# Retiming the small pieces between the layers of a fused two-layer network on one Trainium2 core

## The reference

```
# layer 0: wavelet filters and linear attention, and a gated network
xn   = layernorm(x)
low, highs = two levels of dwconv(4 taps)[:, ::2] on xn
q    = elu(h) + 1;  k = q;  v = h                 # h: low, 16 heads of 16
num  = q (k^T v);   den = q . sum(k) + 1e-6;  low = num / den
low  = synthesis by dwconv of repeated low and highs; y = layernorm(xn + low)
h    = silu(xn W1 s1) * (xn W2 s2)                # 1024 wide
g    = gelu(h H1 s);  g = gelu(g H2 s)            # 1024 x 1024, twice
x2   = x + y * silu(g W3 s)
# layer 1: selective state space with 16 states, feed-forward, 8 experts of which 2
xn   = layernorm(..); delta = softplus(xn Wd + bd); B, C = xn Wbc
h_t  = exp(delta A) h_(t-1) + delta xn B_t;  y_t = h_t . C_t;  s = y + D xn
s   += gelu(layernorm(s) W1 + b1) W2 + b2          # 256 -> 1024 -> 256
nf   = rmsnorm(x');  top 2 of 8 logits, softmax of the two -> combine weights
moe  = sum over chosen experts of mlp2(clipped swiglu(mlp1(nf)))
out  = x2 + s * silu(x' + moe)
```

## Time and profile before

| | before |
|---|---|
| median of 3 runs | 1803.55 us |
| profiled execution | 1803.55 us, its span 1801.8 us |
| PE matmul busy | 1456.6 us (81%) |
| DVE busy | 1386.9 us (77%) |
| ACT busy | 1142.9 us (63%) |
| POOL busy | 973.2 us (54%) |
| mean granted TensorE clock | 0.92 of full speed |

### The profile page before, as it was taken

The page is one execution under the profiler, slowest core; times in us unless marked ns, Lnnn a source line. Parts: engine busy times, 40 slices in busy tenths (PEclk is TensorE's granted clock), DMA queues, the critical chain, the costliest instruction groups (busy, mean ns, idle before and its releaser), DMA issues. The chain is left out here.

```text
span 1801.8 us, 16539 instructions
## 1 busy us (share of the span) xinstructions
PE 1456.6 (81%) x5296; PEld 628.9 (35%) x5296; DVE 1386.9 (77%) x1736; ACT 1142.9 (63%) x1575; POOL 973.2 (54%) x616
## 2 busy tenths in 40 slices
PE   4899889899888789899897779889897764654676
PEld 1354334344333234434343324434343221111232
DVE  2683268899688878889688878989678869989844
ACT  3536678777527668868527668878526754465565
POOL 2132164667009775757008875756107864784854
PEclk9999999999999889999999989999999885686989
DMA  8001000000201000000201000000100200000000
GB/s 197 1 10 50 1 12 1 24 1 1 82 0 36 24 24 1 24 1 0 82 0 36 24 24 1 19 6 1 70 12 15 114 24 0 1 1 0 0 12 12
DMA packets 12600, 42.43 MB, mean 24 GB/s; under 512 B 1866, under 2 KB 1890, under 8 KB 10466
## 3 DMA queue, kind: packets, MB, share of 16 engines
q1 hardware_dynamic: 11698, 35.08, 5.3%
q0 software_dynamic: 816, 6.30, 1.6%
HBM read 38.23 MB, written 4.19 MB: 24 GB/s over the span
## 5 line engine op out<-in xcount | busy, mean ns | idle before, releaser
L795 POOL TENSOR_TENSOR gate<-gate,lin 128x512 f32<-128x512 f32 x120 | 154.8, 1290 | 346.2 <-DVE lin L2407 341.2
L772 POOL TENSOR_TENSOR gx<-gx,sy 128x1024 f32<-128x1024 f32 x120 | 292.7, 2439 | 37.9 <-DVE sy L2288 33.0
L1171 ACT ACTIVATE gate<-gate 128x512 f32<-128x512 f32 x128 | 80.2, 627 | 163.2 <-DVE gate L2396 163.0
L1531 PE MATMUL psf<-g1p,h2w 128*128 128x512 f16 x768 | 182.2, 386 | 0.6 <-ACT tf L958 0.6
L750 POOL TENSOR_TENSOR g2p<-tf,g2p 128x512 fp32r<-128x512 f32 x64 | 86.1, 1351 | 163.7 <-ACT g2p L981 163.7
L2255 DVE TENSOR_TENSOR psu<-so,psu 128x1024 f32<-128x1024 f32 x128 | 156.5, 1223 | 17.8 <-PE psu L1655 17.0
L1078 ACT ACTIVATE da<-delta,aneg 128x512 f32<-128x512 f32 x256 | 163.5, 710 | 4.3 <-DVE st L2272 3.7
L2272 DVE TENSOR_TENSOR_SCAN st<-da,carry,psu 128x512 f32<-128x512 f32 x128 | 156.8, 1267 | 8.4 <-ACT carry L1093 6.6
L1817 PE MATMUL psu<-ap,mw 128*128 128x512 f16 x384 | 109.0, 413 | 54.3 <-POOL ap L800 54.2
L2272 DVE TENSOR_TENSOR_SCAN st<-da,psu 128x512 f32<-128x512 f32 x128 | 149.1, 1206 | 1.9 <-issue 0.3
L800 POOL TENSOR_TENSOR ap<-gate,ap 128x512 f16<-128x512 f32 x116 | 142.9, 1234 | 0.0
(11 more groups left out here) (395 smaller groups left out, 3359.3 us busy)
## 6 DMA issues: line engine op xcount, KB each, us to landing
mw<-in_mlp_w SPq DMA_DIRECT2D x3, 2048.0 KB, 8.0
xn<-in_x SPq DMA_DIRECT2D x8, 512.0 KB, 5.9
wf<-in_wf SPq DMA_DIRECT2D x4, 1024.0 KB, 4.8
xr<-in_x SPq DMA_DIRECT2D x8, 512.0 KB, 3.7
x<-gx SPq DMA_DIRECT2D x8, 512.0 KB, 3.8
out<-outc SPq DMA_DIRECT2D x8, 512.0 KB, 3.1
mw<-in_mlp_w SPq DMA_DIRECT2D x3, 1024.0 KB, 10.1
h1w<-in_h POOLq DMA_DIRECT2D x1, 2048.0 KB, 12.7
```

The source lines that it names most:

```text
L772: pool.tensor_tensor(out, chunk(gx, c), sy[:, n % 2], ALU.add).then_inc(y_acc.sem, 1)
L795: pool.tensor_tensor(gate[:, r % NG], gate[:, r % NG], lin_at(b, r)[:], ALU.mult)\
L1531: last = pe.matmul(banks[m], w[:, t, cols], src[:, half, t], start=(t == 0 and half == 0), stop=(t == KF - 1 and half == 1))
```

## The change

Only numbers change: at which step of a stage some small pieces stand. No instruction's operands change, no DMA moves on SP, and SP's order is the same. The number of ACT's table loads, which follows from the order, goes from 251 to 262.

```diff
@@ constants of the schedule @@
 NEXT_AT, NEXT_CENTER_AT, NEXT_SQ_AT, NEXT_VAR_AT, NEXT_STD_AT, NEXT_SCALE_AT, NEXT_SPLIT_AT, NEXT_LOW_AT = \
-    26, 27, 28, 31, 31, 33, 32, 32
+    26, 27, 28, 29, 30, 32, 33, 33
-LI_AT, LI_SQ_AT, LI_VAR_AT, LI_ROOT_AT, LI_SCALE_AT, LI_SPLIT_AT, LI_LOW_AT = 5, 6, 7, 9, 9, 10, 11
+LI_AT, LI_SQ_AT, LI_VAR_AT, LI_ROOT_AT, LI_SCALE_AT, LI_SPLIT_AT, LI_LOW_AT = 6, 7, 8, 9, 9, 10, 11
 LF_SQ_AT, LF_VAR_AT, RMS_AT, Q_AT, RMS1_AT, ATTN_AT, LOGITS_AT, NUM_AT, EXP_AT, TURN_AT, TURN1_AT = \
-    0, 2, 3, 5, 5, 7, 7, 9, 9, 13, 13
+    0, 2, 3, 4, 5, 6, 7, 8, 9, 10, 12
@@ POOL, batch, expert stage @@
-((10, l0_product, 0), (11, l0_out, 0), (13, l0_product, 1), (16, l0_out, 1))
+((8, l0_product, 0), (10, l0_out, 0), (15, l0_product, 1), (16, l0_out, 1))
@@ ACT, opening, chunk 1 @@
-((7, l0_std, 1), (7, head_root, 0), (9, split_input, 1), (10, head_affine, 0), (13, softplus, 0), (13, head_b16, 0))
+((7, l0_std, 1), (8, head_root, 0), (9, split_input, 1), (10, head_affine, 0), (12, softplus, 0), (13, head_b16, 0))
@@ ACT, batch, expert stage @@
-(24, softplus)
+(23, softplus)
@@ ACT, closing, chunk 0 @@
-((2, head_square, 1), (1, expert_root, 0), ...
+((1, head_square, 1), (1, expert_root, 0), ...
@@ PE, batch, expert stage @@
-(8, lb_average, 1) ... (14, head_mean)
+(7, lb_average, 1) ... (13, head_mean)
@@ PE, closing, chunk 1 @@
-(7, expert_turn, 1)
+(6, expert_turn, 1)
@@ DVE, opening @@
-(2, lb_center, 0)
+(1, lb_center, 0)
@@ DVE, batch, expert stage @@
-(19, head_norm), (21, head_z0)
+(18, head_norm), (20, head_z0)
@@ DVE, closing, chunk 0 @@
-(10, head_softplus)
+(9, head_softplus)
```

More of the change, by code:

```diff
@@ L849, in batch @@
                     if b0 is not None:
-                        for at, piece, c in ((10, l0_product, 0), (11, l0_out, 0), (13, l0_product, 1),
+                        for at, piece, c in ((8, l0_product, 0), (10, l0_out, 0), (15, l0_product, 1),
                                              (16, l0_out, 1)):
@@ L1322, in batch @@
                                     piece(b0, c, wave)
-                            for at, piece in ((14, head_square), (16, head_root), (19, head_affine), (24, softplus),
+                            for at, piece in ((14, head_square), (16, head_root), (19, head_affine), (23, softplus),
                                               (B16_AT, head_b16)):
@@ L1349, in closing @@
                         carry_state(b, n - 1)
-                    for at, piece, c in ((2, head_square, 1), (1, expert_root, 0), (3, head_root, 1), (5, head_affine, 1), (5, head_b16, 1),
+                    for at, piece, c in ((1, head_square, 1), (1, expert_root, 0), (3, head_root, 1), (5, head_affine, 1), (5, head_b16, 1),
                                          (7, softplus, 1)):
@@ L1927, in batch @@
                                     piece(b0, c, wave)
-                            for at, piece in ((14, head_mean), (16, head_var), (20, head_delta0),
+                            for at, piece in ((13, head_mean), (16, head_var), (20, head_delta0),
                                               (22, head_delta1), (24, head_bc)):
@@ L2512, in batch @@
                                     piece(b0, c, wave)
-                            for at, piece in ((14, head_center), (19, head_norm), (21, head_z0),
+                            for at, piece in ((14, head_center), (18, head_norm), (20, head_z0),
                                               (22, head_z1), (24, head_parts), (26, head_softplus),
@@ L2582, in closing @@
                     expert_scale(b, late)
[L2583 removed]
+                    for at, piece in ((8, head_parts), (9, head_softplus), (10, head_late)):
                         if n == at:
```

11 lines of the change are left out of this document (5 added, 6 removed).

## The result

The changed kernel takes 1862.98 us, the median of 4 runs (1860.57 to 1869.87), against 1803.89 before: 1.0334 times as long, 95% interval 1.0304 to 1.0364. That is 59 to 60 us slower. The forecast was 1849 with a range to 1864: the sign was right, the size was short by 14 to 15. The median lies 1 us inside the upper end of the range, and the time by the ratio (1.0334 x 1803.89 = 1864.1) just outside.

The account below looks back on a forecast made before the run. No single engine bounds the kernel; time goes where one instruction stream waits for another. Terms 28.8 + 10.5 + 1.0 + 1.5 + 1.5 + 2.5 = 45.8 us on 1803.55 gave 1849 us, range 1824 to 1864.

Parts of the forecast that it names:

- Hidden stage, 28.8: Hidden stages: PE holes before kv and the second turn make block_out(1) 9.6 us late, three times 28.8 (17 to 34).
- The clock's price of 1.8: Hidden stage: PE's lowered clock after each of the two holes, before kv and the second turn, costs 1.8 us more.
- Its first rival: Slower, but half: TensorE keeps full clock across the new holes, expert stage swallows its part; 24.4 us, 1828; 20%.
- its third: Each table switch costs 1.38 us more where ACT is dense: 2.8 a stage, 8.3 in all, 1858; 7%.
- Expert stage, 10.5 (3 to 15): Expert stages: later head_norm chain on DVE 2.8 us, PE and POOL holes 0.7; 3.5 a stage, bounds 1 and 5.
- That product ends when it ended, since POOL does the same work before it: Expert stage: POOL's l0_out(1), which head_norm waits for, keeps its end time; clip 19 and scale 18 stand behind the wait.
- up to a tile's work: Expert stage: PE waits longer at the earlier head_mean for POOL's l0_out(0); with POOL's short holes, 0.7 us together.
- DVE's own term, 2.8 a stage: Expert stage: head_norm and head_z0 one step earlier on DVE bring clip 22 at 605.6 instead of 602.82, 2.8 us.
- Joint, 1.0 (0 to 4): Joint to next row, twice: ACT's two extra loads mostly lie beside the last tiles; 0.5 us each, 1.0 for both.
- First norm beside the states, 1.5: State stages, three times: mean, square and variance one step later put the square in denser ACT; 0.5 us each, 1.5.
- opening, 1.5: Opening: softplus at step 12 makes ACT's Gelu 2.5 us late, PE's next tile with it; together 1.5 (1 to 3).
- Closing, 2.5: Closing: ACT's square ahead of expert_root and the C-row copy delays PE's C row and DVE's output 2.5 us (0 to 3.5).

Follow-up runs that it names:

- e1: Kernel before with the hidden stage's numbers alone (q_expo 4, attention 6, attention_num 8, turns 10 and 12): 1837.92 us, 1.0175.
- e4: Kernel before with POOL's four expert-stage steps alone (l0_product and l0_out at 8, 10, 15, 16): 1812.17 us, 1.0043.
- e16: Kernel before with POOL's four and DVE's two expert-stage steps plus lb_average(1) at 7; head_mean and softplus as before: 1825.41 us, 1.0112.
- e11: Kernel before with POOL's four and DVE's two expert-stage steps, without PE's averages and ACT's softplus: 1817.50 us, 1.0078.
- e3: Kernel before with DVE's two expert-stage steps alone (head_norm 18, head_z0 20): 1811.94 us, 1.0038.
- e5: Kernel before with the numbers of the next row's first norm alone (variance 29, root 30, scale 32, split and low 33): 1810.12 us, 1.0034.
- e6: Kernel before with the expert stage's edits of POOL, DVE, PE and ACT and the joint's numbers together: 1829.02 us, 1.0133.
- e2: Kernel before with the expert stage's edits of POOL, DVE, PE and ACT, without the next row's norm: 1823.80 us, 1.0100.
- e9: Kernel before with only the edits outside expert and hidden stages: opening, first norm beside the states, closing's head_square: 1808.24 us, 1.0023.

## Why the forecast was right, and where it failed

In short, the mechanism of the hidden stage was right, and the expert stage was mis-sized because POOL's lateness and one edit on PE had been put at nothing.

1. *Hidden stage, 28.8.* Right step by step: in e1 both holes are within 0.1 us, `block_out(0)` and `(1)` within 0.3. The clock's price of 1.8 behind each hole measured in the changed kernel 1.7 behind kv (1.85 - 1.13 and 2.87 - 1.88) and 1.5 behind the turn (0.59 - 0.38 and 3.19 - 1.88). Its first rival (full clock, half the loss) is refuted by these groups, its third (a drain at every load) by ACT's rows: activations start at the end of each load. That the sum came to 28.5 is in part luck. Alone the edits cost 30.5, since the clock takes 1.4 more in the middle batch. In the changed kernel the first batch gives 2 us back (7.8 for 9.6): PE comes to the square's wait later and idles 2.67 instead of 3.18 us, and the four matmuls behind it take 1.98 instead of 3.32. The absolute times of that batch agree with the forecast only because it began 2.2 us late.
2. *Expert stage, 10.5 (3 to 15), measured 28.5: the step that failed.* "That product ends when it ended, since POOL does the same work before it" was wrong. POOL does the same work, but it is fed late and idles 2.3 us ahead of the product at step 15, and both pieces stand behind that. `l0_out(1)` ends 3.8 late, 4.8 in the middle stage, and `head_norm` waits 4.7 instead of the 2.7 that its steps give (0.61 + 2.1). Of these 3.8, POOL's own edits make 1.6 (e4) and the tail of the hidden stage 0.6 (e1); the rest comes with PE's averages. Second, `lb_average(1)` was left out, which put it at nothing without a reason; on top of POOL's and DVE's edits it cost 9.5 in the stages, about 6 in time (e16 against e11). Third, `head_mean` got 0.7 a stage for a wait of "up to a tile's work"; alone it cost 15.7 in the stages, in the set nothing that can be told. DVE's own term, 2.8 a stage and 8.4 in all, was right: 8.3 in e3.
3. *Joint, 1.0 (0 to 4).* Measured 3.7 in the expert stages of e5 and 5.2 beside the other edits (e6 against e2): the loads do not lie "beside the last tiles" but ahead of the last silu.
4. *First norm beside the states, 1.5, and opening, 1.5.* In e9 the state stages are 1.4 to 2.4 longer, no more than unedited ones vary by, and each hidden stage is 1.7 shorter, by the shorter hole just named; in the changed kernel only the first batch has it. The opening shows no change beyond its scatter: the Gelu is late as worked out, but "PE's next tile with it" is not. Together these parts of e9 are 1.2 shorter than before (0.6 + 3.2 - 5.0), where I had 3.0 longer.
5. *Closing, 2.5.* Measured 3.5 and, in e9, 3.75, with the mechanism as written: DVE's output behind the C row is 2.8 late after the first scan. The size is at and beyond the bound of 3.5.
6. *The range.* Its upper terms, 34 + 15 + 4 + 3 + 3 + 3.5, make 62.5 and not 62, which ends at 1866 and not at 1864; and the upper bound of the hidden stage should be 11.8 a stage (two falls of 2.9 for two of 1.8), not 11.5. That the time came so near the range's end is no merit of the expert term, which missed its own bound of 15 by 13.5.

The account of the expert stages: POOL's and DVE's edits 11.8, `lb_average` on top of them 9.5, `head_mean` with the softplus -2.8 (to e2's 18.5), the joint to 23.7, the hidden stage's tail 3.7, together 27.4 of 28.5. It is a sum of differences in this one order, of one profiled execution each; in another order the single terms would differ.

## What to carry to other kernels

Of each piece that moves, write a line, also of the ones that look small: a piece of 1.7 us ahead of one tile cost 6 to 9 us over three stages. Where an engine shows no hole (POOL from 560 to 595), its order is still not free: with three of its pieces moved its second `l0_out` ended 1.6 to 3.1 us later (e4). And prices of single edits need not add. The halves of the hidden stage did, but `head_mean` was 15.7 us alone and nothing in the set. So measure a suspect by taking it out of the full change too.
